# Who counts the first bytes of the last four tiles: GpSimd's three instructions or VectorE's one

## What is computed

```python
x = x + cross_attention(layernorm(x), ctx)          # 2 x 1024 rows of 256
norm = layernorm(x.reshape(2048, 256))
scores = norm @ centroids.T                         # 2048 x 8
taken = zeros(2048, bool)
for e in range(8):                                  # balanced_assignment
    s = where(taken, -inf, scores[:, e])
    _, idx = top_k(s, 256)                          # expert e takes its 256 best free tokens
    taken[idx] = True
# each expert: layernorm, gelu(h @ w1 + b1) @ w2 + b2, added to its rows, rows put back in their places
```

## Time and profile before

| | |
|---|---|
| time, median of 3 executions | 325.0 us (324.57 to 325.73) |
| the profiled execution | 324.3 us, of which the profile's span is 322.5 us |
| PE busy | 289.0 us, 90% of the span |
| DVE busy | 219.2 us, 68% |
| POOL busy | 207.7 us, 64% |
| ACT busy | 145.3 us, 45% |
| mean granted clock of PE | 0.958 |

### The profile page before, as it was taken

How to read it: one execution, slowest core, us unless ns; L and a number is a source line. 1 busy time by engine, 2 the same in 40 slices (tenths; PEclk the granted TensorE clock), 3 DMA queues, 4 the chain that set the end, 5 groups by cost and what they waited for, 6 DMA issues and landing times.

```text
span 322.5 us, 6634 instructions
## 1 busy us (share of the span) xinstructions
PE 289.0 (90%) x2080; PEld 249.2 (77%) x2080; DVE 219.2 (68%) x742; ACT 145.3 (45%) x266; POOL 207.7 (64%) x287
## 2 busy tenths in 40 slices
PE   7999998999999999999811599999999999999990
PEld 4999887999989999999700267787878787878890
DVE  0679999788888887888538867878787878311000
ACT  1366564456545446655441244353535353532420
POOL 8200444468888888887855335758686868787831
PEclk9999999999999999999955599999999999999998
DMA  7993005930001000000112201645555655543010
GB/s 270 352 381 137 2 0 186 378 122 36 33 37 60 33 33 33 33 33 36 65 65 86 91 22 33 187 141 183 177 182 178 189 172 183 182 137 119 17 65 16
DMA packets 21768, 37.76 MB, mean 117 GB/s; under 512 B 2417, under 2 KB 14961, under 8 KB 21361
## 3 DMA queue, kind: packets, MB, share of 16 engines
q1 hardware_dynamic: 19184, 31.15, 28.0%
q0 software_dynamic: 2560, 6.31, 6.4%
HBM read 31.16 MB, written 6.29 MB: 116 GB/s over the span
## 4 chain that ended last, share of the span: by engine, by line
PE 72%; DVE 12%; issue 5%; POOL 5%; DMA 3%; ACT 2%; SPq 0%; POOLq 0%; DVEq 0%
PE pair L1058 63%; PE pair L1134 4%; DVE cmpb L919 3%; PE pair L1108 2%; DVE pair L952 2%; DMA wk_s<-wk_dram 2%; PE pair L1297 2%; POOL yT L499 1%; DMA G<-rows_scratch,idx 1%; POOL atleast L405 1%; PE pair L1146 1%; DVE sm L786 1%; DVE ok L939 1%; DVE wneg L707 1%; POOL sc L423 1%
## 5 line engine op out<-in xcount | busy, mean ns | idle before, releaser
L1058 PE MATMUL pair<-w2s,hT 128*128 128x256 f32 x256 | 63.2, 387 | 0.0
L1058 PE MATMUL pair<-yT,w1p 128*128 128x256 f32 x384 | 53.2, 288 | 1.6 <-POOL yT L499 1.6
L1058 PEld LDWEIGHTS pair<-yT,w1p 128*128 128x128 f32 x384 | 47.6, 188 | 4.3 <-issue 2.1
L1058 PE MATMUL pair<-Bm,pT 128*128 (+1 forms) x384 | 49.3, 283 | 0.2 <-ACT pT L580 0.2
L1058 PEld LDWEIGHTS pair<-w2s,hT 128*128 128x128 f32 x256 | 45.7, 191 | 4.6
L1058 PE MATMUL pair<-Am,xTp 128*128 (+1 forms) x192 | 48.9, 403 | 0.0
L1058 PEld LDWEIGHTS pair<-Bm,pT 128*128 128x128 f32 x384 | 46.1, 188 | 0.4 <-issue 0.4
L667 ACT ACTIVATE hT<-pair,b1s 128x256 f32<-128x256 f32 x64 | 26.9, 471 | 34.1 <-PE pair L1058 32.4
L493 POOL TENSOR_TENSOR w1p<-w1s,w1p 128x512 fp32r<-128x512 f32 x32 | 40.0, 1273 | 3.3 <-ACT w1p L646 3.1
L1058 PEld LDWEIGHTS pair<-Am,xTp 128*128 128x128 f32 x192 | 34.9, 188 | 7.4
L257 POOL TENSOR_TENSOR pr<-pr,rs 128x1024 f32<-128x1024 f32 (+1 forms) x16 | 31.2, 1950 | 14.0 <-DVE rs L793 12.7
(11 more groups left out here) (146 smaller groups left out, 544.9 us busy)
## 6 DMA issues: line engine op xcount, KB each, us to landing
w1s<-w_dram SPq DMA_DIRECT2D x8, 1024.0 KB
w2s<-w_dram SPq DMA_DIRECT2D x8, 1024.0 KB, 7.8
rows_scratch<-row SPq DMA_DIRECT2D x16, 256.0 KB, 2.0
xs<-x_dram SPq DMA_DIRECT2D x1, 2048.0 KB, 17.1
xTs<-xT_dram SPq DMA_DIRECT2D x1, 2048.0 KB, 18.8
wk_s<-wk_dram SPq DMA_DIRECT2D x1, 1024.0 KB, 4.9
wv_s<-wv_dram SPq DMA_DIRECT2D x1, 1024.0 KB, 7.3
wqT_s<-wqT_dram SPq DMA_DIRECT2D x2, 512.0 KB, 8.6
```

The lines of the kernel that those rows point to most:

```text
L1058: return nc.tensor.matmul(out_, l, r, start=start, stop=stop)
```

## The change

The counts of tiles 12, 13 and 14 go from POOL to DVE, so that `first_bytes` is called only inside the pipeline (up to tile 11). DVE counts tiles 12 and 13 after `x1_variance` of tile 14 and ahead of `x1_add` of tile 15, tile 14 between `score(14)` and `score(15)`, and tile 15 after `score(15)` as before. Each count waits for its tile's score and for the count before it. The instruction is the one that tile 15 had.

```diff
--- before.py
+++ after.py
@@ -247,9 +247,6 @@
         def score_bank(t):
             return bank[3] if is_last(t) else bank[7]
 
-        def count_bytes(eng, t):
-
-            return eng.scalar_tensor_tensor(hist[:], dig[:, 0, :], S[:, 0, ds(t, 1)], hist[:], ALU.is_le, ALU.add)
 
         def normalise(eng, v, first, end):
 
@@ -457,9 +454,6 @@
             normalise(nc.gpsimd, (T - 1) % 2, KG // 2, KG).then_inc(s_pn, 1)
             for t in range(T - 3, T):
                 second_norm(t, t % 2)
-                if t < T - 1:
-                    first_bytes(t - 1)
-            first_bytes(T - 2)
 
 
             for v in range(2):
@@ -851,6 +845,14 @@
                     nc.vector.tensor_copy(bcent[:], bank[7][:, C + E:C + 2 * E]).then_inc(s_cent, 1)
             steps(dve, A_FIRST, A_LOOP, A_LOOP_END, DRAIN, attn)
 
+            def count_bytes(t):
+
+
+                dve.wait_ge(s_sc, t + 1)
+                dve.wait_ge(r_hist, t)
+                nc.vector.scalar_tensor_tensor(hist[:], dig[:, 0, :], S[:, 0, t:t + 1], hist[:], ALU.is_le,
+                                               ALU.add).then_inc(r_hist, 1)
+
             x, y, z = T - 1, T - 2, T - 3
             x1_add(z, z % 2)
             score(z - 1, (z - 1) % 2)
@@ -868,14 +870,15 @@
             score(z, z % 2)
             x1_stats(y, y % 2)
             x1_variance(y, y % 2)
+            count_bytes(z - 1)
+            count_bytes(z)
             x1_add(x, x % 2)
             x1_stats(x, x % 2)
             x1_variance(x, x % 2)
             score(y, y % 2)
+            count_bytes(y)
             score(x, x % 2)
-            dve.wait_ge(s_sc, T)
-            dve.wait_ge(r_hist, T - 1)
-            count_bytes(nc.vector, x).then_inc(r_hist, 1)
+            count_bytes(x)
 
 
             dve.wait_ge(s_sc, T)
```

## The result

The changed kernel takes 321.22 us (median of 4, 320.79 to 321.75) against 325.13 us (324.57 to 325.73, 4 executions): ratio 0.9875, 95% interval 0.9859 to 0.9891, a gain of 3.5 to 4.6 us. The forecast was 321.25.

A forecast was written before the change was run, and what follows sets the result against it. POOL's counts around the last norm were taken to bound the seam before the experts. An undisturbed gain of 4.2 us became 3.75 with the hold, so 325.0 - 3.75 = 321.25 us, range 320.2 to 322.8.

The forecast's parts named there:

- The bound: Seam between tiles and experts: POOL's counts delay the last norm by 1.9 us, and its last count is late again.
- The free counts: DVE before x1_add(15): counts of tiles 12 and 13 take about 1.0 us in a 1.77 us gap, cost zero.
- The hold: Last norm: DVE counts reading two SBUF inputs hold POOL and the reverse, cutting the gain from 4.2 to 3.75 us.
- Rival 1: Last norm: no hold between POOL and DVE on such small instructions; gain 4.2 us, time 320.8, chance 0.14.
- my sum: Up to the last count: from 165.98 to 162.23 with the hold, gain 3.75 us; profiled span 318.75 us.
- The shift to the end: Behind the last count: all moves by 3.75 us; row stores and w1_rest stay hidden, token_rows(0) keeping 2.5 us idle.
- Rival 3: Start of the experts: the rows, moving only 1.3 to 1.7 us, set it; time about 323.4, chance 0.06.
- The clock: PE before the experts: full clock returns about 3.4 us after the first keep_busy group, as before; no new cost.
- Rival 2: PE before the experts: clock returns later relative to the work, losing 0.6 to 1.7 us; time 321.9 to 323.0, chance 0.13.
- Rival 4: Experts begin at half clock: 0.5 us lost per us of low clock, gain gone at 7.5 us; chance 0.02.

The follow-up runs named there:

- a1: Changed kernel with only tile 14 counted by DVE, POOL keeping the counts of tiles 12 and 13; 322.37 us, ratio 0.9918 to before.
- a2: Changed kernel with only tiles 12 and 13 counted by DVE, tile 14 staying on POOL behind the last norm; 323.43 us, ratio 0.9953 to before.
- b2: Changed kernel plus four extra count-like DVE instructions behind the counts of tiles 12 and 13, output unchanged; 322.12 us, ratio 0.9915 to before.
- a4: Changed kernel with tile 14's count reading its byte values from a PSUM copy, leaving one SBUF input; 320.97 us, ratio 0.9873 to before.
- b1: Changed kernel plus one extra count-like DVE instruction right behind tile 14's count, output unchanged; 321.95 us, ratio 0.9906 to before.
- c2: Changed kernel with the two additions of the last norm made by DVE instead of POOL; 321.17 us, ratio 0.9879 to before.
- d2: Changed kernel without the keep_busy groups of slot 1, 15 matmuls on ones left out, output unchanged; 322.81 us, ratio 0.9927 to before.
- a3: Changed kernel with tile 14's count moved behind score(15) instead of ahead of it; 321.94 us, ratio 0.9901 to before.

## Why the prediction was right

**The bound.** POOL's two parts, counts in front of the last norm and a count behind it, are shown apart by a1 (2.38 us by A) and a2 (1.82).

**The free counts.** Done at 158.49, x1_add(15) still released by PE with 0.80 us idle. b2 shows that the 1.3 us over it counted.

**The hold.** Right in kind, too large in size. I let count 14 hold L421 (L418 after) and gave it 0.39 us; it was 0.16. Two things were off. I let L420 hold count 14 in turn, so that the count would run from 0.19 to 0.67 us behind the start of `second_norm(15)`. In fact it ran from 0.08 to 0.56: it began at 160.55 while L417 (160.47 to 160.66) still ran. So only 0.29 us of it lay beside L418. And of this overlap 0.13 us wasn't lost. I also let count 15 wait for L425; it didn't, it began 0.04 behind the score's end. And POOL started 0.26 us behind the variance's start where I had 0.32. By the trace the gain of the stretch is 4.14 us (6.11 - 1.97) against my 3.75. The step that was off is the term of the hold: "L421 starts at 160.86 in place of 160.47" and "count 15 starts behind it at 162.23". Rival 1, no hold, gave 4.2, which is nearer to the 4.14 than my sum; but its mechanism is refuted, as a4 shows the hold by taking it away.

**The hit was luck in part.** The median came out at 321.22 for a forecast of 321.25, while the term behind it was 0.4 us too small. The profiled span is 318.6 us, for 318.75 in the sum. There the 0.4 us more of gain was nearly taken back at the start of the kernel: `x1_variance(15)` was 0.34 us later than in the trace before, and PE's first matmuls on `wk_s` already were, at 6.67 us for 6.31 (last section). The median's gain is 3.91 us, and its interval of 3.5 to 4.6 takes in either sum, so the times alone don't tell the forecast from rival 1; the traces do.

The Trainium skill ("SBUF — State Buffer", "Who interferes with whom") names the condition rightly, two SBUF inputs against a GpSimd instruction that reads SBUF: the trace agrees, 0.35 against 0.19 us in a4. That the loser blocks for the whole instruction, and that GpSimd has the pair for its own whole instruction, doesn't agree: the loss was 0.13 us short of the overlap in b1, and in c2 a power of 0.71 us, begun 0.02 ahead, neither delayed nor lengthened the count. There the measurements decide.

**The shift to the end.** C is 133.1 to 133.5 in all kernels but d2, and the first two counts, `w1_rest` and the row stores stayed covered: `token_rows(0)` waited 2.54 us for DVE, for 2.5 forecast. Rival 3 didn't happen.

**The clock.** Rival 2's mechanism is real and lies within the forecast: its distance from the work went from 2.9 to 5.4 us, and cost up to 0.6 us in B, the lower end of the 0.6 to 1.7 that I gave. The changed kernel has 3.1 us in one execution and 5.4 in another, so it belongs to the scatter. Of the kernel before there is one trace, with 3.5; that its executions scatter in the same way is likely and not shown. Rival 4 was priced by d2: at 0.2 to 0.4 us per us of low clock against my 0.5, the gain of 3.9 would need 10 to 16 us of it. Its "Twelve matmuls with 256 columns take 1.33 us" misreads the row, which has nine; twelve take 1.66 (the changed kernel, 187.49), and the estimate of half a us for each us doesn't hang on it. (The Trainium skill, "TensorE: Matmul & The Clock Gate", the clock gate, says that the moment of release varies from run to run; the 3.1 and 5.4 us of one code agree.)

## What to carry to other kernels

Where an engine's queue holds two jobs, one urgent and one that can wait, read when the urgent one's data was there: the distance to its start (here 1.9 us) and what stands behind it are separate gains, and here they added up. An instruction that is free because another engine covers it has a cover with an end: compare it with the idle time that is left. A moved instruction takes its ports with it, so look whether the neighbours are longer in the new trace; here that cost 0.16 us of a gain of 4.1, and an input in PSUM took it away. For differences of half a us, stretches between two fixed events in the trace say more than the medians.

## What the runs showed of the hardware that was not expected

A GpSimd instruction beside a VectorE instruction with two SBUF inputs lost 0.16 us at an overlap of 0.29 (changed kernel) and 0.24 at 0.38 (b1), when it began 0.19 and 0.10 us behind it. In a1 it was 0.09 at 0.23, in b2 0.28 at 0.42, where it began 0.06 behind. L423 of the changed kernel began 0.03 us behind the last count (162.21 against 162.18) and took its 0.19. The other way round, a VectorE count held by GpSimd, none was seen in these traces.

The moment at which PE's clock came back lay 2.9 to 5.4 us behind the total ahead of the first `keep_busy` group, in kernels that have the same instructions on PE from the search on.

A good part of the scatter between these executions arises at the start, before anything of this change: PE's first matmuls on `wk_s` wait for that load. Where the 32 of them took their usual 3.81 to 3.83 us, `x1_variance(15)` follows 153.5 to 153.6 us behind the first, in the kernel before and in all that change nothing ahead of it, whether the first came at 6.31 us or, in a3, at 7.43. The timelines of PE of the changed kernel and of c2 have them at

```profile
6.67 1.58 PE L1061 MATMUL pair<-ctx_s,wk_s 128*128 128x128 f32 x12 [0.98 <-DMA wk_s<-wk_dram]
```

```profile
7.53 0.88 PE L1067 MATMUL pair<-ctx_s,wk_s 128*128 128x128 f32 x3 [1.96 <-DMA wk_s<-wk_dram]
```

and in the kernel before at 6.31. The load of c2 was 0.86 us later, PE sat idle for 1.96 us, and the granted clock fell, as windows of c2 show:

```profile
6.00:8.00 2.00, 0.47 (x3) 0.51 (x4) 0.00 (x0) 0.00 (x0) 2.00 (x5) 0.91 1.01 383
8.00:10.00 2.00, 2.00 (x11) 2.00 (x11) 0.00 (x0) 0.00 (x0) 1.72 (x7) 0.50 1.05 368
10.00:12.00 2.00, 2.00 (x15) 2.00 (x15) 0.00 (x0) 0.60 (x1) 0.00 (x0) 0.74 1.10 364
```

The 32 matmuls on `wk_s` then took 5.44 us where the changed kernel's took 3.81. Together 2.5 us, by which c2's `x1_variance(15)` is later too (162.71 against 160.21). That execution was the longest of its five, 322.86 us against a median of 321.17. So a load that was 0.9 us late cost 2.5 us, 1.6 of it at the low clock. It doesn't always: in a3 PE sat idle for 1.79 us, the clock stayed at full, and the matmuls took 3.81, so that only the lateness of 0.8 us was lost. A scatter of that kind can hide an edit of 0.3.
